# The first stage's product by one level of Strassen's scheme: seven products of halved operands, for two tiles at a time

## What is computed

```
x: (2048, 50, 32)                         # batch b, nodes n, features d
fusion = x.reshape(b, 1600)
adj = einsum('bn,tnm->btm', fusion, masker_param) + masker_bias   # (2048, 2, 2500), contraction over 1600
adj = relu(adj).reshape(b, 2, 50, 50)
adj = adj / (adj.sum(-1) + 1e-6)
m   = einsum('btnm,btmd->btnd', adj, h @ weight)                  # h is x for both t
gates = m @ w_ih.T + b_ih + h @ w_hh.T + b_hh  -> r, z, n ; h = (1-z)*tanh(r*n) + z*h
batch norm over b, layer norm over (t, n, d), softmax-weighted sum over nodes -> (2048, 64)
```

## Time and profile before

| | |
|---|---|
| time, median of 3 runs | 2264.7 us (2263.0 to 2267.82) |
| the profiled execution | 2267.87 us, its span 2266.1 us |
| stage 1 | from the start to about 1460 us |
| busy in the span | PE 97%, PEld 77%, DVE 48%, ACT 42%, POOL 6% |
| DMA | 264 MB, mean 116 GB/s |

### The profile page before, as it was taken

How to read it: one execution, slowest core, us unless ns; L and a number is a source line. 1 busy time by engine, 2 the same in 40 slices (tenths; PEclk the granted TensorE clock), 3 DMA queues, 4 the chain that set the end, 5 groups by cost and what they waited for, 6 DMA issues and landing times. The chain is left out here.

```text
span 2266.1 us, 34747 instructions
## 1 busy us (share of the span) xinstructions
PE 2196.3 (97%) x12302; PEld 1738.1 (77%) x12302; DVE 1086.5 (48%) x2177; ACT 961.4 (42%) x1639; POOL 135.4 (6%) x124
## 2 busy tenths in 40 slices
PE   8999999999999999999999999999999999986888
PEld 6888888888888888888888888777777777772333
DVE  4432233323335233322333133278888888884656
ACT  4322122212224122212222122278888888876551
POOL 0000000000000000000000000011101111004340
PEclk9999999999999999999999999999999999997899
DMA  6411222122224322122220223367676776746440
GB/s 215 154 54 64 94 91 90 29 93 90 90 91 144 107 91 93 43 77 91 95 89 28 93 93 72 103 166 197 187 198 180 194 193 183 200 150 194 119 119 5
DMA packets 341600, 264.00 MB, mean 116 GB/s; under 512 B 169318, under 2 KB 302854, under 8 KB 339846
## 3 DMA queue, kind: packets, MB, share of 16 engines
q1 hardware_dynamic: 323402, 225.63, 34.0%
q10 hardware_dynamic: 18144, 37.69, 5.1%
HBM read 195.59 MB, written 67.70 MB: 116 GB/s over the span
## 5 line engine op out<-in xcount | busy, mean ns | idle before, releaser
L443 PE MATMUL psum<-w_hi,x_lo 128*128 128x500 f32 x2080 | 821.2, 395 | 8.9 <-DVE w_lo L292 8.9
L443 PE MATMUL psum<-w_lo,x_hi 128*128 128x500 f32 (+1 forms) x2080 | 808.4, 389 | 0.0
L443 PE MATMUL psum<-w_hi,x_hi 128*128 128x500 f32 x1920 | 744.2, 388 | 0.0
L355 DVE TENSOR_REDUCE rows<-u 128x10 f32<-128x500 f32 x160 | 107.6, 673 | 889.6 <-ACT u L305 889.1
L443 PEld LDWEIGHTS psum<-w_hi,x_lo 128*128 128x128 f32 x2080 | 391.6, 188 | 83.7 <-issue 8.2
L443 PEld LDWEIGHTS psum<-w_lo,x_hi 128*128 128x128 f32 (+1 forms) x2080 | 391.9, 188 | 72.2
L443 PEld LDWEIGHTS psum<-w_hi,x_hi 128*128 128x128 f32 x1920 | 361.0, 188 | 73.0
L311 ACT COPY at<-psum 125x512 f32<-125x512 f32 x160 | 93.5, 585 | 676.4 <-PE psum L425 676.4
L305 ACT ACTIVATE u<-psum 128x500 f32<-128x500 f32 x160 | 93.8, 586 | 344.3 <-PE psum L443 344.3
L764 PE MATMUL psum<-adj_sb,xs_sb 100*64 100x100 f32 x2048 | 200.6, 350 | 1.6 <-PEq L145 1.6
L744 POOL TENSOR_TENSOR xg_lo<-xg_sb,xg_hi 128x400 fp32r<-128x400 f32 x64 | 67.0, 1050 | 1927.5 <-ACT xg_hi L593 1927.5
(11 more groups left out here) (162 smaller groups left out, 2277.8 us busy)
## 6 DMA issues: line engine op xcount, KB each, us to landing
w_raw<-W SPq DMA_DIRECT2D x140, 500.0 KB, 7.9
adjT<-at SPq DMA_DIRECT2D x160, 250.0 KB
adj_sb<-adjT SPq DMA_DIRECT2D x32, 1250.0 KB
xs_sb<-xz SPq DMA_DIRECT2D x16, 1600.0 KB
hF<-hC ACTq DMA_DIRECT2D x96, 256.0 KB, 6.5
h<-hF SPq DMA_DIRECT2D x64, 256.0 KB, 4.2
xg_sb<-xg ACTq DMA_DIRECT2D x14, 800.0 KB, 8.0
h<-hF SPq DMA_DIRECT2D x48, 192.0 KB, 3.5
```

The costliest lines, as they stand in the source:

```text
L355: nc.vector.tensor_reduce(rows[:, 0], u[:, c2], AX.X, ALU.add).then_inc(dve_step, 1)
L443: last = nc.tensor.matmul(mm_out(w % 2), a[0:r, w, k, :], b[0:r, k, :], start=k == 0 and n == 0, stop=k == KF and n == 1)
```

## The change

Two tiles (A over B) are taken together as a matrix of 2 x 2 blocks: the rows are the two tiles, the contraction is halved into 800 and 800 (6 chunks of 128 and a rest of 32 each). The weights of a group are halved in the contraction too, and in the columns (250 and 250). By the Strassen-Winograd scheme seven products of such halves replace eight. The operands are, on the side of x, A11, S2, A12, A21 (S3), S1, A22 and S4, on the side of the weights B11, T2 (kept in B11), B21, T3 (kept in B22), T1 (in B12), T4 (in B21) and B22 as loaded a second time (F22). A product of one slot takes 18 matmuls of 250 columns and one packed one: 19, where one tile and one group took 38 of 500.

- Two pairs of tiles are worked on at a time, in two slots, with the same weights. A step G is one group for both slots (4 tiles): 14 products and 16 transposes. There are 40 steps, in 8 segments of 5; at the end of a segment one slot gets a new pair. So the weights of a group are split and summed 40 times, before 20.
- The weights' operand goes through a ring of three buffers `w_op` (`RING`, 7 operands on 3 buffers). `w_hi` on ACT and `w_lo` on DVE fill it in two units (750 columns; 750 and a part of 250).
- Sums of the weights (`t1` to `t4`) are four GpSimd instructions of 128x1750 for each step; the sums of x (`s_add`) are four of 128x896 for each new pair, on GpSimd (on DVE for the first two pairs).
- The seven products are put together on DVE by 14 additions of 128x250 for a step (`add`, one operand in PSUM, the other in SBUF); ACT only copies the first product (`p1`). The relu then runs in SBUF, 128x1000 at a time; `scale`, the last part of the normalising, moves from DVE to GpSimd.

```diff
--- before.py
+++ after.py
-UNITS = [(u, min(u + 2, KC)) for u in range(0, KC, 2)]
...
+OPS = 7
...
+SLOTS = 2
...
+RING = (0, 1, 2, 0, 1, 2, 1)
+BEHIND = (4, 2, 4, 3, 3, 3, 2)
...
+X_OF = (A11, S2, A12, A21, S1, A22, S4)
...
+W_OF = (B11, B11, B21, B22, B12, B21, F22)
...
+            def load_w(q, G):
+
+                if q == B22:
+                    wait(sp, w_ready, 2 * OPS * (G - 1) + 8 if G else 0)
+                elif q == B12:
+                    wait(sp, w_ready, 2 * OPS * (G - 1) + 10 if G else 0)
+                elif q == B11:
+                    wait(sp, t4_done, G)
+                elif q == B21:
+                    wait(sp, w_ready, 2 * OPS * (G - 1) + 12 if G else 0)
+                else:
+                    wait(sp, w_ready, 2 * OPS * G)
+                    wait(sp, t1_done, G)
+                sp.dma_start(raw[q][:], wq[group_of(G), q if q < 4 else B22]).then_inc(w_loaded[q], 16)
...
+        def t3(eng, V, G):
+
+            eng.wait_ge(w_loaded[B22], 16 * (G + 1))
+            eng.wait_ge(w_loaded[B12], 16 * (G + 1))
+            V.tensor_tensor(raw[B22][:], raw[B22][:], raw[B12][:], ALU.subtract).then_inc(t3_done, 1)
+
+        def t2(eng, V, G):
+
+            eng.wait_ge(w_ready, 2 * OPS * G + 2)
+            eng.wait_ge(t3_done, G + 1)
+            V.tensor_tensor(raw[B11][:], raw[B22][:], raw[B11][:], ALU.add).then_inc(t2_done, 1)
...
+            def w_lo(G, i, unit):
...
+                c = slice(3 * unit, 3 * unit + 3)
+                last = V.tensor_tensor(o[:, LO + 3 * unit:LO + 3 * unit + 3, :], s[:, c, :], o[:, c, :].bitcast(fp32), ALU.subtract)
+                if unit:
+                    last = V.tensor_tensor(o[2 * HR:KLAST, PK, :], s[2 * HR:KLAST, HF, :], o[2 * HR:KLAST, PK, :].bitcast(fp32),
+                                           ALU.subtract)
+                last.then_inc(w_ready, 1)
...
+            def add(G, p, i, out, other, after=0):
...
+                V.tensor_tensor(out, bank(p, RING[i]), other, ALU.add).then_inc(dve_read[p], 1)
...
+            def normalise(G, side):
+
+                dve.wait_ge(relu_done[side], G + 1)
+                wait(dve, norm_done[side], G)
+                r = rows[:, side]
+                sync(V.tensor_reduce(r, both(side), AX.X, ALU.add))
+                sync(V.tensor_scalar_add(r, r, EPS_ROW))
+                V.reciprocal(r, r).then_inc(rows_ready[side], 1)
...
+        @block.gpsimd
+        def _(pool):
+            V = nc.gpsimd
+
+            def t1(G):
+
+                pool.wait_ge(t2_done, G + 1)
+                pool.wait_ge(t3_done, G + 1)
+                pool.wait_ge(w_loaded[F22], 16 * (G + 1))
+                V.tensor_tensor(raw[B12][:], raw[F22][:], raw[B11][:], ALU.subtract).then_inc(t1_done, 1)
+
+            def t4(G):
+
+                pool.wait_ge(w_ready, 2 * OPS * G + 6)
+                V.tensor_tensor(raw[B21][:], raw[B21][:], raw[B11][:], ALU.subtract).then_inc(t4_done, 1)
+
+            def scale(G, side):
+
+                pool.wait_ge(rows_ready[side], G + 1)
+                V.tensor_tensor(both(side), both(side), rows[:, side].unsqueeze(2).to_broadcast([P, SLOTS * GN, N]),
+                                ALU.mult).then_inc(norm_done[side], 1)
+
+            for seg, j, G, g in steps():
+                t1(G)
+                t4(G)
+                if 1 <= j <= 3 and seg + 1 < SEGS:
+                    for which in ((1, 2), (3,), (4,))[j - 1]:
+                        s_add(pool, seg + 2, which)
+                if G < LAST:
+                    t3(pool, V, G + 1)
+                    t2(pool, V, G + 1)
+                    scale(G, SIDE_B)
+                    scale(G, SIDE_A)
...
+            def product(G, i, p, x_count, first=False):
...
+                for unit in range(2):
+                    pe.wait_ge(w_ready, 2 * t + unit + 1)
+                    for k in range(3 * unit, 3 * unit + 3):
+                        for n, (ka, kb) in enumerate(((LO + k, k), (k, LO + k), (k, k))):
+                            last = nc.tensor.matmul(out, a[:, ka, :], b[:, kb, :], start=k == 0 and n == 0, stop=False)
+                    if unit == 0 and p == 1:
+                        last.then_inc(w_used, 1)
+                r = KLAST + 1 if i in K_ONES else 3 * HR
+                nc.tensor.matmul(out, a[0:r, PK, :], b[0:r, PK, :], start=False, stop=True).then_inc(done[p], 1)
```

More of the change, by code:

```diff
@@ L299, in _ @@
+            for p in range(SLOTS):
+                sp.wait_ge(done[p], OPS * LAST + 2)
+            load_xs(sp, shared, ins, 0)
+            for p in range(SLOTS):
+                sp.wait_ge(done[p], OPS * LAST + 3)
+            load_xg(sp, shared, ins, 0)
+            for q in range(4):
+                store(LAST, q)
         @block.scalar
         def _(act):
-            def relu(c, c2, start=False):
-                act.wait_ge(mm_done, c + 1)
-                if not start:
-                    act.wait_ge(an_ready, c - 1)
-                nc.scalar.activation(u[:, c2].rearrange("p n m -> p (n m)"), mm_out(c2), ACT.Relu).then_inc(u_ready, 1)
@@ new lines, in _ @@
+            x_lo(0, 0)
+            w_lo(0, 0, 0)
+            w_lo(0, 0, 1)
+            s_add(dve, 0, 1)
+            s_add(dve, 0, 2)
+            x_lo(0, 1)
+            x_lo_rest = iter(range(2, OPS))
+            t3(dve, V, 0)
+            t2(dve, V, 0)
+            s_add(dve, 0, 3)
+            s_add(dve, 0, 4)
+            for op in x_lo_rest:
+                x_lo(0, op)
+            w_lo(0, 1, 0)
+            w_lo(0, 1, 1)
+            for which in (1, 2, 3, 4):
+                s_add(dve, 1, which)
@@ new lines, in group @@
+            def group(G, x_counts, first=False, second=False):
+                for i in range(OPS):
+                    for p in range(SLOTS):
+                        product(G, i, p, x_counts[p], first)
+                        if first:
+                            if (i, p) == (1, 1):
+                                pe.wait_ge(shared.weights_loaded, 64)
+                                nc.tensor.matmul(g_bank, shared.wT4[:], shared.wih[:], start=True, stop=True).then_inc(g_product, 1)
+                                pe.wait_ge(ident_loaded, 16)
+                            if (i, p) == (3, 1):
+                                pe.wait_ge(blocks_ready, 1)
+                        else:
+                            for q, place_ in enumerate(((0, 1), (1, 0), (1, 1), (2, 0))):
+                                if (i, p) == place_:
+                                    turn(G - 1, q, start=second and q < 2)
@@ L485 @@
+            for seg in range(SEGS):
+                counts = (OPS * (seg // 2), OPS * ((seg + 1) // 2))
+                base = seg * SEG
+                if seg == 0:
+                    group(0, counts, first=True)
+                    group(1, counts, second=True)
+                with pe.Fori(2 if seg == 0 else 0, SEG) as j:
+                    group(base + j, counts)
+            for q in range(4):
+                turn(LAST, q)
 SETS = [(n, list(range(n, FC, QC))) for n in range(QC)]
```

607 lines of the change are left out of this document (312 added, 295 removed).

## The result

The changed kernel takes 2800.4 us (median of 4 runs, 2796.3 to 2802.48), the kernel before 2265.55 us beside it (4 runs, 2263.0 to 2267.82). The ratio is 1.2359, 95% interval 1.2338 to 1.238: 535 us slower. The forecast was 2632 us, so the direction and the mechanism held in the main, and the size was 168 us short; the measured time lies at the upper edge of the stated range of 2400 to 2800 (0.4 us beyond it) and 20 us above the walk's own 2500 to 2780.

A forecast was written before the change was run, and what follows sets the result against it. PE's matmuls bound stage 1 before; afterwards DVE and POOL blocking each other would hold PE up. 2266.1 + 276 (steps) + 57 (segments) + 30 (start) + 3 (stage's end) = 2632 us; range 2400 to 2800.

The forecast's parts named there:

- the walk: One stage 1 step followed through DVE, POOL and PE: 42.9 us, 6.9 more than before; as a case, chance 0.64.
- What bounds before: Stage 1 of the kernel before is bound by PE's matmuls, 36.0 us for four tiles and one group.
- Matmuls of 250 columns: Stage 1's matmuls of 250 columns start 0.12 us apart, making a step 33.7 us on PE.
- the rival at 0.225: Matmuls of 250 columns cost up to 0.225 us, a step 61.7 us, total 3330 us; chance 0.03.
- DVE and POOL exclude each other: In stage 1, DVE operations with two SBUF inputs and POOL instructions hold each other up; shared way taken 31.7 to 36.3 us a step.
- One sign named beforehand: DVE, blocked time counted, is busy for over 80% of stage 1.
- B12, whose load goes out after the `w_lo` of operand 4 ... it lands at about 0: In a step, `t3`'s weights load takes 7 us and lands at about the end of product 4, time 0.
- the clock: PE restarting at the 1.2 GHz level after idling nearly 6 us costs up to 3.6 us a step, giving 46.5.
- the changes of segment: Splitting and summing a new pair in 7 of 8 segments costs 8 us each, 57 in all (0 to 120).
- The start: At the kernel's start, product 0 of slot 1 begins near 40 us, costing 30 us more.
- PE stays the bound: Rival: DVE and POOL interleave so no blocked piece reaches PE, total 2217 us; chance 0.08.
- Packed tight: Rival: the shared SBUF way bounds a step at 37 to 39.8 us, total 2340 to 2450; chance 0.18.

The follow-up runs named there:

- e9: e4 with loads and `w_lo` reordered, and T1 and T3 stored in the first ten steps and loaded afterwards: 2264.0 us, ratio 0.9993 to the kernel before.
- e3: Changed kernel with GpSimd's six operations of a step cut to 8 columns each, all waits kept: 2364.0 us.
- e4: Changed kernel with all sums and both scalings moved from GpSimd to VectorE in stage 1: 2497.4 us.
- e1: Changed kernel with the second store put ahead of B22's load in SP's queue: 2688.8 us, ratio 1.1866 to the kernel before.
- e11: e9 with the stores of T1 and T3 issued by GpSimd and an earlier start: 2248.8 us, ratio 0.9913 to the kernel before.
- e6: e1 with `t1` also held on GpSimd until `w_lo` of operand 1 is written: 2662.3 us.

## Why the prediction was nearly right, and where it fell short

- *What bounds before:* right. Only a shorter step on PE could gain, and e9 shows that 3.15 us is what there was.
- *Matmuls of 250 columns:* I took 0.12 us. e9's 140 us hold 64 transposes (16 x 0.45 = 7.2 us) and 1140 matmuls: 0.116 us. Right, and the rival at 0.225 is refuted. PE alone needs 32.85 us a step, predicted 33.7.
- *DVE and POOL exclude each other:* right, and the main cause of the loss. `w_lo` has the two kinds, POOL's sums last 3.96 us undisturbed and 4.6 to 4.7 when begun during a DVE operation, PE's idle time is ended by `w_lo` L447 and L445. Without POOL's work (e3) 10.4 us a step go away, with it on DVE (e4) 7.2. Sized a little off: POOL's sum 3.75 for 3.96, its scaling 2.25 for 1.87. One sign named beforehand came out short: DVE is busy for 79% of stage 1 (1490 of 1897 us), not for over 80%.
- *The walk, 42.9 us a step:* its order around `w_lo` 1 held, its price didn't: 47.1. **The first step that failed is "B12, whose load goes out after the `w_lo` of operand 4 ... it lands at about 0".** I gave each load its semaphore and its 7 us, and never walked SP's queue, in which the load stands behind three stores, and the last of these behind ACT's copy and the landing of an earlier store. Over the 21 steps that touch no change of segment, `t2` begins 11.5 us behind the end of product 4 and not at 8.6, and `w_lo` 1 is done at 26.6 and not at 24.3. e1 measures the late loads at 2.8 us a step; in it `t2` begins at 8.8 and `w_lo` 1 is done at 23.9, as walked.
- **The second is the clock, priced at up to 3.6 us a step and then left out of the 42.9.** From the end of `w_lo` 1 to the end of product 4 the walk has 18.6 us, the changed kernel takes 20.5 and e1 20.3. In the step at 577 us PE starts again at 576.97 and the granted clock is 0.50 until 582.1, which is 2.6 us lost, and matmuls at 0.116 for 0.12 win some 0.6 back. 2.3 us late and 1.9 us on PE are the 4.2. No run holds the clock and changes nothing else, so this second part is read from the trace alone.
- *The other terms, up to stage 2:* predicted 366 us, measured 487.7. 39 step distances 4.2 us longer are +164; the changes of segment cost 31 and not 57, -26; the last four steps, with less to prepare, are 16 shorter: together +122, the whole difference. The two terms that were too large, by 42 us together, hid part of the miss; that is luck. The start was right: slot 1's product 0 begins at 40.95, predicted near 40.
- *Stage 2:* predicted unchanged, in fact 39.5 us longer. Nothing in the profile of before shows it; only the changed kernel's own loop could.
- *The rivals:* "PE stays the bound" needed GpSimd to block for under 7 us a step, and it gave 2217. e9 to e11 get there by taking GpSimd's sums out, and even then reach only 2249. For e11 the account up to stage 2 is 39 distances of 3.15 us less, -123; the first nine +49, the later changes of segment and the last four steps +22, and the rest, start and end, +32: about -20, where stage 2's start is 19.2 us earlier. "Packed tight", 37 to 39.8 us a step, would need SP's order and a DVE queue that never waits; e6, the best with GpSimd at work, has 43.6.

Where the expected gain of one level of the scheme went: 126 us saved on PE; taken back by GpSimd's part (10.4 us a step with SP's order as it is: the exclusion, its own durations and the clock together), by late loads (2.8 to 3.3), by the start, and by 39.5 us in stage 2 that have nothing to do with the scheme.

## What to carry to other kernels

When work is moved to an idle GpSimd, count its time as time in which VectorE's operations on SBUF inputs stand, not as time beside it: where both read two inputs from SBUF, a faster VectorE doing all of it (1.98 us for 3.96) won here by 7.2 us a step. A walk of a step must include the queue that issues the DMAs, store by store, with what each store waits for. Idle time of PE that the walk predicts has a second price, the clock at which PE goes on, and it belongs in the sum. And compare two kernels stage by stage before explaining a total: a stage whose source is untouched can change because its code has moved.

## What the hardware showed that I had not expected

- VectorE stood for 6.3 to 6.7 us behind a loop's branch back, with no releaser in the timeline but with packets of an `instruction` DMA queue in the round; with 144 instructions more ahead of the loop 5.9 and 4.3 us; with the loop written out not at all. One round took 78.3 us in place of 70.2.
- The exclusion doesn't scale with the blocked operation: 33x250, 0.42 us by itself, lasts 4.01 us, as long as GpSimd's sum of 1750 columns. The scalar addition of 128x20 has 0.18 and 0.88 us. An addition with one input in PSUM, 128x250, stayed at 0.42 us or less in all 560 instances.
- GpSimd's sum of 128x1750 took 3.94 to 3.99 us, VectorE's 1.98 us: 2.26 against 1.13 ns a column.
- Matmuls of 250 columns, each with its own weight load, started 0.116 us apart, hardly more than half of the 0.225 of 500 columns.
